# Where the high part of the next gate weights stands in ScalarE's tile loop: a routed feed-forward kernel on one core

## The reference, cut to what matters

```python
y = x @ W_base.T + lora(x)                      # 2048 tokens, 512 wide; lora picked by batch
probs = softmax(y @ gate_w.T); top 2 of 16 experts per token
g = einsum('th,eih->tei', y, w_gate)            # INTER = 352
u = einsum('th,eih->tei', y, w_up)
h = silu(g) * u
out = x + sum over the 2 experts of weight * (h @ w_down.T)
```

## Time and profile before

| | us |
|---|---|
| median of three executions | 355.73 |
| profiled execution | 356.19 |
| its span, first to last instruction | 354.3 |
| TensorE busy | 337.6 (95%) |
| VectorE busy | 233.0 (66%) |
| ScalarE busy | 179.4 (51%) |
| mean granted TensorE clock | 0.987 of full |
| chain that ended last: share on TensorE | 76% |

### The profile page before, as it was taken

One profiled execution on the slowest core, in us unless ns is written; L12 is line 12 of the kernel. 1 busy time (PEld: TensorE's weight loads), 2 busy tenths in 40 slices (PEclk: granted clock), 3 DMA queues, 4 the chain that ended last, 5 costly groups with the idle time before them and its releaser, 6 DMA issues.

```text
span 354.3 us, 7808 instructions
## 1 busy us (share of the span) xinstructions
PE 337.6 (95%) x1879; PEld 298.3 (84%) x1879; DVE 233.0 (66%) x307; ACT 179.4 (51%) x242; POOL 134.1 (38%) x85
## 2 busy tenths in 40 slices
PE   8999999999996998999999999999999999999990
PEld 4777878779886997999899998999989998899970
DVE  0576799986634538485778858788586678778310
ACT  1498622522445463555467554674545476564320
POOL 0000000023527732418374665766645452226231
PEclk9999999999998999999999999999999999999996
DMA  7994865639296899699999995999969789920422
GB/s 277 395 480 134 318 240 177 242 132 335 68 322 137 237 302 310 178 306 281 274 274 303 310 306 160 282 321 266 293 172 285 212 244 293 251 34 4 59 35 37
DMA packets 47352, 82.22 MB, mean 232 GB/s; under 512 B 5488, under 2 KB 22000, under 8 KB 47216
## 3 DMA queue, kind: packets, MB, share of 16 engines
q1 hardware_dynamic: 38336, 62.70, 53.8%
q0 software_dynamic: 8960, 18.89, 23.4%
HBM read 60.59 MB, written 19.92 MB: 227 GB/s over the span
## 4 chain that ended last, share of the span: by engine, by line
PE 76%; DMA 13%; DVE 3%; issue 3%; SPq 2%; ACT 1%; POOLq 1%; DVEq 0%; ACTq 0%
PE bank L690 35%; PE bank L719 19%; DMA xs<-xg 4%; PE bank L546 4%; PE bank L550 4%; PE bank L547 4%; DMA out<-ys,sidx 4%; DMA xg<-y_rows,gidx 3%; PE bank L446 3%; PE bank L664 3%; DMA head_sb<-head 2%; SPq L427 1%; PE bank L477 1%; PE bank L573 1%; DMA y_rows<-y_st 1%
## 5 line engine op out<-in xcount | busy, mean ns | idle before, releaser
L1244 POOL DMA_INDIRECT out<-ys,sidx x40 | 81.4, 2034 | 119.5 <-DMA out<-ys,sidx 56.6
L1223 POOL DMA_INDIRECT xg<-y_rows,gidx x40 | 52.2, 1305 | 94.7 <-issue 79.9
L354 DVE TENSOR_TENSOR w_lo<-w_raw,w_hi (+2 forms) x32 | 76.2, 2383 | 11.9 <-issue 8.1
L690 PE MATMUL bank<-w_hi,xt_hi 128*128 x320 | 82.5, 334 | 0.2 <-issue 0.2
L690 PE MATMUL bank<-w_hi,xt_lo 128*128 x320 | 79.3, 325 | 0.0
L690 PE MATMUL bank<-w_lo,xt_hi 128*128 x320 | 79.3, 324 | 0.0
L352 ACT ACTIVATE w_hi<-w_raw (+2 forms) x32 | 64.6, 2020 | 11.0 <-DMA w_raw<-wall 8.9
L844 ACT ACTIVATE sg<-bank 128x352 f32<-128x352 f32 x40 | 18.5, 462 | 77.0 <-PE bank L690 77.0
L690 PEld LDWEIGHTS bank<-w_lo,xt_hi 128*128 128x128 f32 x320 | 56.4, 190 | 0.0
L690 PEld LDWEIGHTS bank<-w_hi,xt_lo 128*128 128x128 f32 x320 | 56.4, 190 | 0.0
L690 PEld LDWEIGHTS bank<-w_hi,xt_hi 128*128 128x128 f32 x320 | 55.1, 191 | 1.5 <-issue 0.8
(11 more groups left out here) (181 smaller groups left out, 364.7 us busy)
## 6 DMA issues: line engine op xcount, KB each, us to landing
w_raw<-wall SPq DMA_DIRECT2D x16, 1408.0 KB, 7.7
w_raw<-wall SPq DMA_DIRECT2D x16, 768.0 KB, 9.1
xs<-xg SPq DMA_DIRECT2D x128, 64.0 KB
x_st<-xin SPq DMA_DIRECT2D x8, 512.0 KB, 13.0
y_rows<-y_st SPq DMA_DIRECT2D x16, 256.0 KB, 4.0
head_sb<-head SPq DMA_DIRECT2D x2, 640.0 KB, 5.1
wb_sb<-wb SPq DMA_DIRECT2D x2, 512.0 KB, 8.8
wbt_sb<-wbt SPq DMA_DIRECT2D x2, 512.0 KB, 10.7
```

The costliest lines, as they stand in the source:

```text
L354: e.tensor_tensor(w_lo[:, bass.ds(dst, n)], raw, hi, ALU.subtract).then_inc(own, 1)
L690: mm = e.matmul(bank[2 + 2 * s + t % 2][:, 0:INTER], a, w[:, bass.ds(at + (k * GU + s * INTER), INTER)], start=k == 0 and i == 0, stop=k = ...
L1223: e.indirect_dma_start(out=xg[t % NXG][:], out_offset=None, in_=y_dram, in_offset=bass.IndirectOffsetOnAxis(ap=gidx[:, t:t + 1], axis=0)). ...
L1244: e.indirect_dma_start(out=out, out_offset=bass.IndirectOffsetOnAxis(ap=sidx[:, t:t + 1], axis=0), in_=ys[t % NYS][:], in_offset=None, bou ...
```

## The change

Three reorderings; no instruction that computes is added or removed. (1) ScalarE's high split of the gate/up weights of tile t+2 moves from before `silu(t)` to after `silu(t)` and `x_evac(t+2)`. (2) VectorE loads the word of tile t+2 right after `product(t)`; before it loaded the word of tile t+1 at the start of iteration t. (3) SyncE's `later_weights(3)` stands ahead of `rows_apart(8)`; before it stood behind it. The other calls keep their order.

```diff
@@ SyncE
-            for t in range(NTILE + N_COPY):
-                if N_PE <= t < NTILE:
+            for t in range(N_PE - N_COPY + 1):
+                later_weights(t)
+            for t in range(N_PE, NTILE + N_COPY):
+                if t < NTILE:
                     rows_apart(t)
-                if 0 <= t - N_COPY < NTILE - NRAW:
+                if N_PE < t < NTILE - NRAW + N_COPY:
                     later_weights(t - N_COPY)
@@ ScalarE
-                    if t + 2 < NTILE:
-                        split_weights(e, count, t + 2, ahead, "gu", a_gu)
                     if t < NTILE:
                         silu(t)
                     if N_PE <= t + 2 < NTILE:
                         x_evac(t + 2)
+                    if t + 2 < NTILE:
+                        split_weights(e, count, t + 2, ahead, "gu", a_gu)
                     if t + 1 < NTILE:
                         split_weights(e, count, t + 1, word, "dn", a_dn)
@@ VectorE
+            ahead = tile_word(e, 3)
             with ExitStack() as rest:
                 for t in range(2, NTILE + 1):
                     go_on(e, rest, count, t - 1)
-                    here = word
-                    if t + 1 < NTILE:
-                        word = tile_word(e, t + 1)
+                    here, word = word, ahead
...
                     if t < NTILE:
                         product(t)
+                    if t + 2 < NTILE:
+                        ahead = tile_word(e, t + 2)
                     if N_PE <= t + 2 < NTILE:
                         y_low(t + 2)
```

## The result

The changed kernel takes 364.95 us (median of 4 runs, 364.11 to 365.43). The kernel before, run beside it, takes 356.18 us (355.64 to 357.31). The ratio is 1.025, with an interval of 1.021 to 1.029. The forecast was 364.1 with a range of 357.5 to 367.5. The profiled execution has a span of 363.5 us, where before had 354.3.

What follows compares the result with a forecast made beforehand. TensorE was taken as the bound, busy throughout the middle, so only holes could win. Terms -3.3 - 0.25 + 9.0 + 3.0 gave +8.4 us: 364.6 from the profiled 356.19, 364.1 as median; range 357.5 to 367.5.

Steps and rivals of the forecast that it cites:

- TensorE's tile has little slack: In a middle tile with a gate split, hh has 0.43 us of slack; a hole costs 0.2 us more for the restart.
- `ht_hi` at 3.93, `h_turn` at 9.0 after silu: Where gate weights are split, ht_hi comes 1.25 us later and the next h_turn starts at 9.0 instead of 8.17.
- Nine experts, 9.0 us: In the middle, each of nine experts' gate splits costs a 0.8 us hole plus 0.2 restart: 9.0 us lost.
- The tail, 1.25 + 0.55 + 1.2 = 3.0: From 285 us on, three experts' splits delay h_turn of tiles 32, 34 and 36: 3.0 us lost, bounds 2.0 and 3.3.
- The first hole, a gain of 3.3: The 3.43 us hole before h_turn(3) goes, half returns at h_turn(4): gain 3.3 us, bounds 1.6 and 5.2.
- Tile 7, a gain of 0.25: At h_turn(7) the old late-copy cause (1.25 us) goes and the moved split's 1.0 us comes: gain 0.25 us.
- SyncE, 0: Issuing later_weights(3) ahead of tile 8's copies makes those copies 3 to 5 us later; cost 0 to 0.5 us, taken as 0.
- Rival A: VectorE reads ahead, so its split follows ht_lo by 0.43 instead of 0.97 us: +1.3 us, about 357; chance 0.1.
- Rival B: TensorE has a hidden reserve of 0.8 us for hh, so the nine holes vanish: 351.2 us; chance 0.1.
- Rival C: Small holes pull TensorE's clock down, each of 13 bringing 3.4 us at half clock: 386 us; chance 0.04.

Runs made afterwards that it cites:

- four kernels of the table: Kernel before with an extra unread ScalarE copy of 256, 768 or 1504 elements in tiles 8 to 29, and the changed kernel: ratios 1.000, 1.010, 1.030, 1.025.
- the middle alone: Kernel before with ScalarE's gate split moved behind silu and xt_hi in iterations 8 to 29 only: 365.73 us, ratio 1.026.
- the extra operation: Kernel before plus an unread ScalarE copy between ys and ht_hi in tiles 8 to 29, of 256, 768 or 1504 elements: 356.05, 359.75, 366.86 us.

## Why the prediction was right, point by point

- **TensorE's tile has little slack.** It held. I read a slack of 0.43 and charged 0.2 for the restart, which leaves 0.23 free. The four kernels of the table put the free part at 0.22 to 0.25. They don't separate the two terms. The holes show 0.64 where 1.0 is lost, because TensorE's busy time grows as well (135.52 in the middle after, 132.41 before). So the hole's length alone would have undercounted the loss by a third.
- **`ht_hi` at 3.93, `h_turn` at 9.0 after silu.** Measured 3.90 and 8.97. The pace came from the down split, which already stood in that place.
- **Nine experts, 9.0 us.** Measured 9.04 in the middle, and 8.85 with the middle alone.
- **The tail, 1.25 + 0.55 + 1.2 = 3.0.** Measured by the length of tiles 32, 34 and 36 (6.85, 7.00 and 6.31 before, 8.18, 7.51 and 7.50 after): 1.33, 0.51 and 1.19; 3.05 over the stretch. That tile 34 came out right is partly luck. I put 1.45 for ScalarE's part and gave back 0.9 for the word load of 1.07 us. That load was an outlier of one execution: with ScalarE's part alone, where it took 0.40 us, tile 34 takes 7.95, which is 1.25 to 1.52 over the 6.43 to 6.70 of the kernels that keep the old order there, so the 1.45 holds. The earlier word gives back 0.44 (7.95 to 7.51), not 0.9; the rest of the 0.9 is a long load that didn't come again. In tile 36 ScalarE's part costs 1.54 and the word gives 0.35, where I had 1.45 less 0.25 for load and slack.
- **The first hole, a gain of 3.3.** Tiles 3 and 4 take 18.71 us before and 15.69 after, a gain of 3.02. The hole at `h_turn(4)` is 1.72 where I had written about 1.5, since the weights landed 0.38 us later in the tile loop's own time (107.10 - 79.18 against 106.16 - 78.62). No half clock followed. I had chosen that between two bounds without a row for a hole of this length.
- **Tile 7, a gain of 0.25.** Measured 0.50 (7.60 to 7.10). The term was half as large as it should be: the new hole is 0.43 there, less than in the middle, and I don't know why.
- **SyncE, 0.** As a sum against the change this was right, and the copies came 4.2 us later (116.20 for 112.03), within the 3 to 5 that I had put. But the reason was only half of it. I asked what the new order costs and not what the old one would cost beside ScalarE's part. The run of ScalarE's part alone shows it: 4.9 us more in tile 7 and the half clock behind it. Had the change left SyncE alone, my forecast (about 364) would have been more than 6 us too low. The 0.25 that I gave for the removal of tile 8's cause was the only sign of it in the sum.
- **Rival A** (VectorE reads ahead) fell: `ht_lo` to split is 0.98 after, 0.97 before, although the word is now loaded a tile earlier. VectorE's sequencer ran the branches of line 337 from 151.2 to 151.6, not before `ht_lo` started at 151.23. The Trainium skill (Perfetto Trace Analysis, section DVE / Act Engine Instruction) has the sequencer ready for the next instruction once a waiting one is in the wait queue. By that rule the 0.42 us of issue ahead of the split would lie under VectorE's 1.62 us wait for `ht_hi`, and the trace after doesn't show it.
- **Rival B** (0.8 us hidden) fell to the table above: what is free, 0.22 to 0.25 us, is what the rows gave, and nothing is hidden on top of it.
- **Rival C** (the clock) fell: clock 1.00 in all three stretches with fourteen holes of up to 1.72 us. The Trainium skill (TensorE: Matmul & The Clock Gate, section A second HAM failure mode) has frequent short idling between groups make the clock oscillate. Nine holes of 0.62 to 0.83 us within 141 us did not do so here.

The sum, +8.4, met the loop's 8.44 more closely than the rows deserve. The first hole gave 0.3 less than forecast and tile 7 0.25 more. The one profiled execution of before also has a longer front and a longer tail than the four kernels that share both with it (those of the extra operation and the swap in iterations 8 to 29): 73.42 against 72.03 to 73.28, and 51.57 against 50.98 to 51.25. The medians moved by 8.8. The term that carries the forecast, nine experts at 1.0 us, doesn't hang on this.

What stays open: why the same hole sometimes brings 3.4 and sometimes 6.8 us at half clock, and whether the 0.25 us is slack or slack and restart.

## What to carry to other kernels

An operation that is moved behind a short one on a busy helper engine has to be costed at each place where it runs, not at the one where it was late: here, of fourteen splits that changed places, one gained 3 us and twelve lost 12. Measure the slack of a tile in which nothing waits; in this kernel lateness beyond it was paid one for one, also where the holes in the trace look shorter than the loss. And where a transfer is late, look at which transfer is needed next, because making the first one early may only hand the wait on.

## What was not expected of the hardware

With the first hole of about 3 us the granted clock went to 0.50, its 1.2 GHz level. In the profiled run of before it stayed there for 3.4 us, all of them under work. In the profiled runs of VectorE's word alone, of SyncE's order alone and of the swap in iterations 8 to 29, which do the same work up to there, it stayed for about 6.8 us (the stretches 108.70:112.10 and 112.10:115.50 above). In these three it fell while TensorE was still idle, so that about 5.4 of the 6.8 us lay under work in the first of them. Tiles 3 and 4 take 19.32 us there and 18.71 before, with a hole that is 0.31 shorter, so the longer stretch costs 0.9 us more.

The kernel before spreads over 4.8 us from run to run (354.23 to 358.98 in the 33 runs beside the experiments). The kernels without any stall of over 2 us spread over 1.5 or less in four runs each (349.27 to 349.71, 351.57 to 353.01, 362.11 to 362.57, 364.11 to 365.43), the other six experiments of four runs over 2.0 to 4.4. So a hole of this length costs steadiness too. The clock has a part in it: of the 33 runs the twelve with a mean granted clock of 0.982 or less have a median of 357.3 us, the other 21 have 355.5. It is not all of it, since the slowest run, 358.98, has 0.984. Whether it comes from a longer stretch at half clock in those runs was not shown.
